# Ids turned into row offsets on ScalarE, and compares on VectorE with constants, in a recommendation tower

## The reference

```python
e = jnp.stack([tbl_0[ids[:, 0]], ..., tbl_26[ids[:, 26]]], axis=1)
dot = jnp.einsum('bnd,bmd->bnm', e, e)
z = dot.reshape(2048, 27 * 27)[:, idx]
h = jnp.concatenate([z, dense_ctx], axis=1)
h = jnp.maximum(h @ W_top1 + b_top1, 0.0)
h = jnp.maximum(h @ W_top2 + b_top2, 0.0)
y = h @ W_top3
```

## Time and profile before

| | |
|---|---|
| median of 3 runs | 383.13 us (382.71 to 384.81) |
| the profiled execution, its own time | 381.17 us |
| its span | 379.3 us |
| granted TensorE clock | 0.987 |
| busy: TensorE, weight loads, VectorE, ScalarE, GpSimd | 345.7, 322.6, 294.4, 153.3, 269.3 us |
| compares (L537) | 658, 205.4 us, mean 383 ns |
| gathers (L379) | 278, 0.96 us each in the mean |

### The profile page before, as it was taken

The page is one execution under the profiler, slowest core; times in us unless marked ns, Lnnn a source line. Parts: engine busy times, 40 slices in busy tenths (PEclk is TensorE's granted clock), DMA queues, the critical chain, the costliest instruction groups (busy, mean ns, idle before and its releaser), DMA issues.

```text
span 379.3 us, 9954 instructions
## 1 busy us (share of the span) xinstructions
PE 345.7 (91%) x4035; PEld 322.6 (85%) x4035; DVE 294.4 (78%) x821; ACT 153.3 (40%) x217; POOL 269.3 (71%) x287
## 2 busy tenths in 40 slices
PE   1788868599999999999999999999999999999985
PEld 1677767588999999998999999998999999998874
DVE  4986696898688969798689969798689869793432
ACT  3352644434343453534343453534243453533421
POOL 6777877777777777777777777777777777777400
PEclk9989996999999999999999999999999999999999
DMA  6995225953333333334333333333343343221100
GB/s 184 251 247 136 64 63 137 213 186 96 82 93 85 79 84 82 95 69 95 82 94 85 79 86 81 95 72 91 85 91 85 76 89 83 76 57 50 36 2 1
DMA packets 22988, 36.38 MB, mean 96 GB/s; under 512 B 6224, under 2 KB 17120, under 8 KB 22944
## 3 DMA queue, kind: packets, MB, share of 16 engines
q0 software_dynamic: 8896, 18.24, 20.2%
q1 hardware_dynamic: 14048, 17.52, 18.6%
HBM read 35.73 MB, written 0.01 MB: 94 GB/s over the span
## 4 chain that ended last, share of the span: by engine, by line
PE 75%; POOL 14%; issue 5%; DMA 3%; ACT 2%; DVE 1%; ACTq 0%; DVEq 0%
PE embT_ps L410 35%; PE gram_ps L442 13%; POOL emb L379 12%; PE h_ps L470 11%; PE h_ps L494 7%; PE embT_ps L420 6%; DMA emb<-in_tbl,idx 3%; PE flat_ps L453 2%; POOL flatT L379 2%; ACT embT L634 1%; DVE flat L568 1%; DMA idx<-in_idx_rows 0%; PE h_ps L481 0%; PE flat_ps L481 0%; DVE flat L569 0%
## 5 line engine op out<-in xcount | busy, mean ns | idle before, releaser
L379 POOL DMA_INDIRECT emb<-in_tbl,idx x272 | 261.8, 962 | 83.8 <-issue 80.6
L537 DVE TENSOR_SCALAR one_hot<-ids,row_of 125x256 fp32r<-125x256 int32 x658 | 205.4, 383 | 13.2 <-PE embT_ps L410 10.6
L410 PE MATMUL embT_ps<-one_hot,tbl 125*128 125x256 f32 x1284 | 182.0, 297 | 13.0 <-DVE one_hot L537 11.4
L410 PEld LDWEIGHTS embT_ps<-one_hot,tbl 125*128 125x128 f32 x1284 | 166.7, 196 | 17.9 <-issue 8.9
L634 ACT COPY embT<-embT_ps 128x256 f32<-128x256 f32 x77 | 48.0, 624 | 134.2 <-PE embT_ps L410 129.0
L642 ACT COPY embT<-embT_ps 128x512 f32<-128x512 f32 (+1 forms) x80 | 80.7, 1012 | 11.7 <-PE embT_ps L420 11.7
L568 DVE STREAM_TRANSPOSE flat<-gram_ps 128x864 f32<-128x864 f32 x31 | 33.5, 1082 | 43.7 <-PE gram_ps L442 43.1
L442 PEld LDWEIGHTS gram_ps<-embT 128*59 128x59 f32 x1984 | 56.2, 134 | 9.6 <-ACT embT L634 3.9
L442 PE MATMUL gram_ps<-embT 128*59 128x54 f32 x1984 | 60.2, 217 | 3.8 <-ACT embT L634 2.3
L420 PE MATMUL embT_ps<-ident,emb 128*128 128x128 f32 x272 | 43.8, 276 | 11.6 <-DMA emb<-in_tbl,idx 8.6
L420 PEld LDWEIGHTS embT_ps<-ident,emb 128*128 128x128 f32 x272 | 32.2, 142 | 13.8 <-DMA emb<-in_tbl,idx 11.4
(11 more groups left out here) (47 smaller groups left out, 85.0 us busy)
## 6 DMA issues: line engine op xcount, KB each, us to landing
ids<-in_ids_hot SPq DMA_DIRECT2D x77, 128.0 KB
emb<-in_tbl,idx POOLq DMA_INDIRECT x272, 3.1
embT<-in_tbl SPq DMA_DIRECT2D x5, 448.0 KB
w_sb<-in_tbl SPq DMA_DIRECT2D x3, 560.0 KB
w_sb<-in_W_ring SPq DMA_DIRECT2D x1, 756.0 KB
w_sb<-in_W_top SPq DMA_DIRECT2D x1, 512.0 KB
h1T<-in_tbl SPq DMA_DIRECT2D x1, 448.0 KB
w_sb<-in_tbl SPq DMA_DIRECT2D x1, 448.0 KB
```

Source lines behind the costliest of these rows:

```text
L379: pool.indirect_dma_start(gathered_row(t, s), None, tables[f][:, :], bass.IndirectOffsetOnAxis(ap=idx[:, t, f:f + 1], axis=0),).then_inc(g ...
L410: mm = pe.matmul(out[:, 0:HN], tbl[0:ROWS, part, AT[o] + chunk, :], one_hot[0:ROWS, k % SLOTS, c, :], start=(chunk == 0 and part == 0), st ...
L537: done = dve.tensor_scalar(one_hot[0:ROWS, k % SLOTS, c, :], of, row_of[0:ROWS, KINDS.index(CH[o]), chunk:chunk + 1], None, ALU.is_equal)
```

## The change

Before the compares of a hot step, ScalarE takes its 256 ids in place from the number of the partition's first row of that table: bias `row_of[p, kind, 0]`, scale −1, so that each value is 8p − id (or 10p − id), as a float. VectorE then compares the float values with the constant −chunk, where it compared integer ids with a per-partition scalar from `row_of`. This holds for all 77 steps (RELATIVE = len(HOTS)), so the old form remains in the text alone. The compares wait for ScalarE's semaphore `ids_relative`, and ScalarE waits for the load. ScalarE does steps 0, 1 and 2 between the first three splits, and step n + 3 at hot step n, behind a split that is due and ahead of the copy of the product. On SyncE, the ids of step 0 are loaded ahead of the first table.

```diff
+    RELATIVE = len(HOTS)
...
             sp.dma_start(idx[:, 0, :], idx_rows[:, 0, :]).then_inc(idx_first, 16)
+            load_ids(0)
             for o in range(SHARED + 1):
                 load_table(o)
-                if o < len(HOT0):
+                if 0 < o < len(HOT0):
                     load_ids(o)
...
                 of = ids[0:ROWS, n % IDS, :]
-                dve.wait_ge(ids_loaded[n % IDS], 16 * (n // IDS + 1))
+                if n < RELATIVE:
+                    dve.wait_ge(ids_relative, n + 1)
+                else:
+                    dve.wait_ge(ids_loaded[n % IDS], 16 * (n // IDS + 1))
...
-                        done = dve.tensor_scalar(one_hot[0:ROWS, k % SLOTS, c, :], of,
-                                                 row_of[0:ROWS, KINDS.index(CH[o]), chunk:chunk + 1], None,
-                                                 ALU.is_equal)
+                        columns = one_hot[0:ROWS, k % SLOTS, c, :]
+                        if n < RELATIVE:
+                            done = dve.tensor_scalar(columns, of.bitcast(F32), float(-chunk), None, ALU.is_equal)
+                        else:
+                            done = dve.tensor_scalar(columns, of, row_of[0:ROWS, KINDS.index(CH[o]), chunk:chunk + 1],
+                                                     None, ALU.is_equal)
...
+            def relative_ids(n):
+
+                act.wait_ge(ids_loaded[n % IDS], 16 * (n // IDS + 1))
+                if n == 0:
+                    act.wait_ge(rows_ready, len(KINDS))
+                kind = KINDS.index(CH[HOTS[n][2]])
+                act.activation(ids[0:ROWS, n % IDS, :].bitcast(F32), ids[0:ROWS, n % IDS, :], ACT.Identity,
+                               bias=row_of[0:ROWS, kind, 0:1], scale=-1.0).then_inc(ids_relative, 1)
...
             AHEAD = 3
+            relative_ids(0)
             for o in range(AHEAD):
                 split_high(o)
+                if o > 0:
+                    relative_ids(o)
             for kind, *of in ORDER:
                 if kind == "hot":
                     n = READ["hot", of[0], of[1]]
...
                         split_high(SPLIT_AT[n])
+                    if n + AHEAD < RELATIVE:
+                        relative_ids(n + AHEAD)
                 if kind == "quad":
```

More of the change, by code:

```diff
@@ L281, in dlrm_tower @@
         low_ready = sem("low_ready")
+        ids_relative = sem("ids_relative")
         ids_loaded = [sem(f"ids_loaded{b}") for b in range(IDS)]
```

## The result

The median went from 383.02 us (11 runs, 379.02 to 384.81) to 387.15 us (11 runs, 384.82 to 390.92). The ratio is 1.0122, 95% interval 1.0088 to 1.0156. The profiled execution took 387.15 us with a span of 385.3 us, so it lies on the median; that of before, 381.17 with a span of 379.3, is 1.9 under its own. The forecast was slower, 387.8, and that is what came. How it came is another matter: beside the cause that was forecast stands a second one, to which the prediction gave 0.06 and which by itself costs as much.

What follows compares the result with a forecast made beforehand. Gathers were taken to bound the kernel until 81 us, then TensorE while gathers keep ahead. Terms 4.4 + 1.5 − 1.2 = +4.7 us gave 385.9 for the profiled execution, median 387.8; range 380.8 to 395.5.

Steps and rivals of the forecast that it cites:

- The compares: VectorE's 658 compares: 0.25 us for 0.34, from start to start 0.17 for 0.26; 66 us less of VectorE, nearly all off the path.
- The second estimate: VectorE's compares, from the Trainium skill's formula: 194 ns each at two elements a cycle, following at about 0.11 us.
- The gathers: GpSimd's gathers under denser compares wait for short holds of the shared path: 0.04 us on 110 gathers, +4.4 us.
- Rival (a): Nothing reaches GpSimd's gathers: the new rhythm misses their start, or the constant is no faster; −1.2 to +1.5, 383 us; chance 0.29.
- The subtractions: Ten subtractions for tables' low parts, where gathers are the path: gathers lose 5.6 us where now 4.1, so +1.5.
- TensorE's gain: Steady part: TensorE waits 3 us in all for late compares; only 0.8 and 0.4 get through, −1.2 us.
- The step that failed: ScalarE's new wait for ids ahead of its copies: covered by 2.04 us of idling, so nothing; uncovered, 8 us.
- Rival (c): ScalarE late: its new wait for ids holds the copy ahead of the dots, up to +8, 391 us; chance 0.06.
- Rival (d): A gather waits for whole compares, 0.12 us on average and 0.12 more to start, on 110 gathers: +26, 409 us; chance 0.03.
- G: Theory tested by the follow-up runs: the denser compares make GpSimd's gathers longer; the forecast's own cause, chance 0.50, +2 to +13.
- S: Theory tested by the follow-up runs: ScalarE's wait for ids behind the table loads holds TensorE; the prediction put this wait at nothing.
- the upper bound: High end for gathers slowed by compares: 110 × 0.13 = 14 us, less the 1.2 that TensorE gains.

Runs made afterwards that it cites:

- run with integers: Against the changed kernel: VectorE compares integer ids with the constant, ScalarE does nothing new, the partition's first row is left out; 387.85 us, ratio 1.0135.
- the one with the tile `minus`: Against the changed kernel: VectorE's scalar is a column of a small tile, the same value in every partition, not the constant; ScalarE's work stays; 387.21 us, ratio 1.0136.
- alternating run: Against the kernel before: first 20 steps unchanged; from step 20 on, ScalarE's new work, with compares taking constant and tile column in turn; 383.06 us, ratio 1.0006.
- Pieces of the subtraction: Against the kernel before: only each subtraction for a table's low part is cut into pieces of two chunks (256 elements); 381.87 us, ratio 0.9969.
- the ids ahead of the tables: Against the changed kernel: table loads that a subtraction releases are issued two steps later, layer 1 weights one step later; 388.94 us, ratio 1.0148.

## Why the prediction was right, and where it was not

- **The compares**: 0.25 us and 0.17 from start to start were predicted; measured 0.28 and 0.20. Six to a gather, as predicted. The 66 us less of VectorE are 48. The small copy's 0.14 was a fair row to start from, but the slope of 0.46 ns per element between two unlike instructions gave 0.03 too little. The run with integers and the one with the tile `minus` show that it is the scalar alone, constant or column, 0.06 us. The second estimate, 194 ns, is 0.09 too low.
- **The gathers**: the mechanism holds. Steady gathers under compares last 1.02 to 1.03. A mean of +0.04 on 110 gathers, 4.4 us, was predicted; it was +0.08 on 71 of them and little on others, 5.3 us more than before between 85 and 340 us. The term was a little small, because the rhythm locks: what happens to one gather happens to its neighbours, and no average over moments applies. The hold of 0.13 us per compare was right: no compare adds more than that to a gather. What the prediction didn't have is that the hold comes 0.06 us earlier in a compare with a constant, so that a start 0.07 ahead, harmless with a column, is not harmless any more. Rival (a) counted on a rhythm that misses the gathers' start; the alternating run has one, with the help of its other form.
- **The subtractions**: 5.6 us, +1.5, was predicted; nine gathers lost 4.9 us behind subtractions, where five had lost 4.1, so +0.8. The early gathers as a whole lost 2.3 more than before; the rest is compares, and one predicated copy of 0.5. Pieces of the subtraction free most of those gathers, so the reading of the earlier trace rows holds.
- **TensorE's gain**: 0.4 us in two tiles, seen to the tenth (42.17 for 42.58). The prediction let only 1.2 us of it through, and this too is about what came before the gathers ran out: 1.3.
- **The step that failed** is the one on ScalarE, "Its wait for the ids is covered if they have landed", and "So nothing". It was worked out for one place, the tightest of the steady part (168 to 173 us). There it nearly holds: from 100 to 345 us no wait of ScalarE for ids is over 0.9 us. It was not worked out for the stretch with table loads and splits, where the ids land in 4.9 and 6.2 us behind a table, not in the 3.1 taken from a gather, and where the compares that release them stand behind a subtraction that ScalarE itself must feed. There it is uncovered three times: ScalarE stands still for 9.35, 9.03 and 6.52 us. With the ids ahead of the tables, 3.15 of the 6.2 us by which TensorE began late are gone, and by itself this wait costs 1.36%, 5 us. Rival (c) named the mechanism and put it "ahead of each tile's dots"; at 0.06 it was far too rarely believed. The activation's own 0.5 us was right (507 ns), and so were the 38 us for all (39.1), though ScalarE is busy only 28 us more.
- **Rival (d)**, a gather waiting for whole instructions: compares lengthen gathers by 0.13 at most, and +26 us did not come. The Trainium skill, page "SBUF — State Buffer", section "SBUF: two separate sides", gives the pair of ports to whoever starts first for the whole instruction. The traces nearly agree, for compares too, but not at the two ends. In all ten profiled executions used here a gather is held until 0.11 to 0.13 us ahead of the recorded end of the compare, the subtraction or the predicated copy: 6.69 + 1.98 − 0.94 = 7.73, and 6.62 + 1.23 − 0.12 = 7.73. And a gather isn't held if it starts 0.01 us behind the start of a compare or a subtraction. Rival (d) let a gather wait for the compare's end and 0.12 us more, which is 0.25 us too long; that, and not the lock, is what made it 26 us.
- **The sum**: +4.7 us, and the medians differ by 4.1; 385.9 was predicted for a profiled execution, 387.15 measured. For G the number is no luck: the kernel that has G alone costs 1.35%, 5.2 us. For the whole change it is luck, because S was put at nothing and is hidden behind G. Had S been seen, adding some 6 us for it to the 4.7 would have given a worse number, 392. The time was right with half of its reasons. (The range was to hold the upper bound, 14 − 1.2 above 383.1; that is 395.9 and 0.4 outside.)

What stays open: why a gather needs the path at its start only for a moment, which part of it holds a compare back towards the end, and why a compare with a column holds the path 0.06 us later, isn't settled. No run changed the period of the compares and kept their form. Nor was a version tried that removes both G and S from the whole change.

## What to carry to other kernels

Where a wait is moved to another engine, follow what releases it through every phase of the kernel, not through the steady part alone: if that leads back to work queued behind the new wait, the two engines go round in a circle and each landing is paid in full. An engine that isn't the bound can be made faster and the kernel slower, if its instructions share a path with one that is full; then try to mix the forms of the instructions, or to cut the long ones, before giving up the speed. And when two causes are each sufficient, undo each one alone: neither undoing shows a gain, and keeping each one alone shows both.

## What the runs showed of the hardware

- A compare of 256 elements with a constant takes 0.28 us, 0.20 from start to start; with a column of a tile as the scalar 0.34 and 0.26. Integer or float ids make no difference (304 and 305 ns on average).
- Gathers and compares lock into a rhythm, of four compares to a gather with the slow form, five when alternating, six with constants. A compare with a constant that starts 0.04 to 0.08 us ahead of a gather makes it 1.02 to 1.05 instead of 0.94 (88 of 88 gathers of the changed kernel); with a column the same start makes nothing (44 of 44 in the alternating run), and one 0.09 to 0.18 ahead makes 1.07 to 0.98. A compare of either form that starts up to 0.02 ahead makes nothing.
- A gather is held until 0.11 to 0.13 us ahead of the recorded end of the VectorE instruction, be it a compare of 0.28 or 0.34 us, a subtraction of 0.42, 1.23 or 1.49, or a predicated copy of 0.77.
- A predicated copy (two inputs, 351 elements) 0.05 us ahead of a gather made it 1.54 us. Subtractions of 1024 elements made one of 1.98, while of eleven gathers behind pieces of 256 elements six lasted 0.94 or 0.95 and the longest 1.12.
